# Attention and mixture-of-experts block on one core: two small operations per tile move to GpSimd, the shared weights are split earlier, the padding goes out in one DMA per expert, and the last experts are split at later places

## The reference

```python
x = x + xattn(ctx, ctx, layernorm(x))       # 16 heads of 16, 64 context rows a batch, softmax, Wo, bias
x = x + ffn(layernorm(x))
# ffn, on z = layernorm(x), n = 2048 rows:
shared = (sum over 2 shared experts of gelu(z @ sw1 + sb1) @ sw2 + sb2) / 2
gates  = z @ router_w + router_b            # 8 experts, the two highest of each row are kept
probs  = softmax(two highest)
moe    = sum over the two of probs * (gelu(z @ w1[e] + b1[e]) @ w2[e] + b2[e])
ffn    = shared + moe
layernorm(x) = (x - mean) / sqrt(var + 1e-5)
```

## Time and profile before

| what | value |
|---|---|
| median of 3 runs | 378.89 us (376.57 to 379.51) |
| the profiled execution, its own time | 380.21 us |
| its span, first to last instruction | 378.5 us |
| mean granted TensorE clock | 0.965 of full speed |
| PE busy | 326.7 us (86%) |
| DVE busy | 238.4 us (63%) |
| ACT busy | 223.0 us (59%) |
| POOL busy | 184.1 us (49%) |
| DMA | 36.93 MB, mean 98 GB/s |

### The profile page before, as it was taken

How to read it: one execution, slowest core, us unless ns; L and a number is a source line. 1 busy time by engine, 2 the same in 40 slices (tenths; PEclk the granted TensorE clock), 3 DMA queues, 4 the chain that set the end, 5 groups by cost and what they waited for, 6 DMA issues and landing times.

```text
span 378.5 us, 8163 instructions
## 1 busy us (share of the span) xinstructions
PE 326.7 (86%) x2306; PEld 275.1 (73%) x2306; DVE 238.4 (63%) x504; ACT 223.0 (59%) x407; POOL 184.1 (49%) x230
## 2 busy tenths in 40 slices
PE   4979998875888999983798999998999999999940
PEld 3757766643657878872787897997989999988830
DVE  0589999999826467870566546665666666666530
ACT  1265578756576866731566457666677677676530
POOL 4326799999632587767000001454534544535540
PEclk9998999999899999998599999999999999999995
DMA  8960000060000923346741303354453553554231
GB/s 263 404 240 3 3 0 31 28 237 0 3 2 4 351 78 135 119 144 186 275 154 55 127 0 73 57 85 75 69 86 72 73 86 70 73 86 72 29 43 14
DMA packets 23930, 36.93 MB, mean 98 GB/s; under 512 B 4400, under 2 KB 18096, under 8 KB 23504
## 3 DMA queue, kind: packets, MB, share of 16 engines
q1 hardware_dynamic: 16000, 25.06, 20.1%
q0 software_dynamic: 7456, 10.04, 15.7%
q10 hardware_dynamic: 432, 1.31, 0.9%
HBM read 23.21 MB, written 13.19 MB: 96 GB/s over the span
## 4 chain that ended last, share of the span: by engine, by line
PE 57%; DVE 10%; DMA 8%; issue 8%; POOL 6%; ACT 5%; SPq 3%; ACTq 0%; DVEq 0%; POOLq 0%
PE psS L1102 12%; PE psP L1127 11%; PE psS L1053 8%; PE psS L967 5%; PE psP L967 5%; DMA out<-xres,xg 4%; PE psS L1114 3%; POOL Pr L423 2%; PE psP L1028 2%; PE psD L902 2%; PE psS L918 2%; DVE mx L777 1%; DMA wraw<-in_w 1%; SPq L264 1%; PE psD L1003 1%
## 5 line engine op out<-in xcount | busy, mean ns | idle before, releaser
L470 POOL DMA_INDIRECT out<-xres,xg x39 | 61.0, 1563 | 58.5 <-DVE xres L869 41.2
L825 DVE TENSOR_TENSOR h_lo<-g,h_hi 128x512 fp32r<-128x512 f32 x32 | 22.1, 692 | 51.7 <-ACT h_hi L573 37.3
L1127 PE MATMUL psP<-w_lo,h_hi 128*128 x156 | 47.2, 303 | 3.3 <-DVE h_lo L877 3.3
L855 DVE TENSOR_TENSOR sraw<-psS,b1T 128x512 f32<-128x512 f32 x39 | 27.0, 692 | 33.2 <-PE psS L1114 32.2
L1127 PE MATMUL psP<-w_hi,h_hi 128*128 x156 | 43.8, 281 | 0.0
L1127 PE MATMUL psP<-w_hi,h_lo 128*128 x156 | 43.7, 280 | 0.0
L570 ACT ACTIVATE g<-psS,sb1T 128x512 f32<-128x512 f32 x32 | 22.0, 687 | 32.6 <-PE psS L1053 32.2
L423 POOL TENSOR_TENSOR Pr<-Pr,inv 128x1024 f32<-128x1024 f32 x16 | 31.3, 1954 | 19.6 <-DVE inv L814 19.6
L608 ACT ACTIVATE g<-sraw 128x512 f32<-128x512 f32 x39 | 24.6, 632 | 26.3 <-DVE sraw L855 26.2
L1102 PE MATMUL psS<-w_lo,xt_hi 128*128 x78 | 34.3, 439 | 1.2 <-issue 1.1
L600 ACT ACTIVATE sraw<-psS 128x512 f32<-128x512 f32 x39 | 23.3, 598 | 20.2 <-PE psS L1102 20.2
(11 more groups left out here) (197 smaller groups left out, 934.5 us busy)
## 6 DMA issues: line engine op xcount, KB each, us to landing
wraw<-in_w SPq DMA_DIRECT2D x16, 512.0 KB, 6.1
xg<-xg_d SPq DMA_DIRECT2D x39, 130.0 KB, 2.1
sraw<-in_sw SPq DMA_DIRECT2D x2, 1024.0 KB, 10.7
out<-xres SPq DMA_DIRECT2D x4, 512.0 KB, 3.4
xres<-in_x SPq DMA_DIRECT2D x3, 512.0 KB, 9.1
xTs<-in_xT SPq DMA_DIRECT2D x3, 512.0 KB, 9.8
xg_d<-filler SPq DMA_DIRECT2D x8, 128.0 KB
s_free<-in_b SPq DMA_DIRECT2D x1, 1024.0 KB, 4.7
```

Source lines behind the costliest of these rows:

```text
L470: pool.indirect_dma_start(out, bass.IndirectOffsetOnAxis(ap=xg[:, t % NXB, D:D + 1].bitcast(U32), axis=0), y[:, t % NYB], None, compute_op ...
L825: V.tensor_tensor(out=h_lo[:, n % 2], in0=g[:, n % 2], in1=h_hi[:, n % 2].bitcast(F32), op=ALU.subtract).then_inc(hlo_done, 1)
L855: V.tensor_tensor(out=hb[:, n % 2], in0=four(hT_bank[n % 2]), in1=b1T[:, bass.ds(e, 1), :].squeeze(1).unsqueeze(2).to_broadcast([P, HC, P] ...
L1127: last = T.matmul(res_bank[n % 2], a[:, n % 2, c * P:(c + 1) * P], b[:, bass.ds(e, 1), C * HF + c * D:C * HF + (c + 1) * D].squeeze(1), st ...
```

## The change

- `ve1`, `ve2` and `nm2` are made on POOL, right before the powers; DVE's `variance` and the two operations of each pair are gone. POOL waits for DVE's `mv1` and `mv2`.
- ACT makes `s_hi` from step 2, POOL `s_lo` from step 3.
- The filler tile has the spare row's index in its own column 256; `pad_row` and its DMA are gone. SP issues eight padding DMAs, and waits for them only before the gathers of the routed tiles. The waits of SP for the padding, for POOL's fillers and for `lean` ahead of expert 5's load are gone; ACT waits for both kinds of padding ahead of its first copy for expert 5, which overwrites `filler`.
- The pieces of experts 5, 6 and 7 go to chunks 19 and 20, 23 and 24, 27 and 28 on ACT (17 and 19, 22 and 23, 25 and 26 before); the last four on DVE to 28 and 29 (27 and 28 before).
- POOL scatters three tiles a step instead of two in steps 20 to 22.

Left out below are the lists of names that lose `pad_row`, and a count of constants that goes from 20 to 19 on PE.

```diff
--- before.py
+++ after.py
@@ -52,8 +52,8 @@
 HALF_T, HALF_G = NT // 2, NG // 2
 NYB, NX, NB = 6, 3, 3
 SPLIT_X = {5: 1, 10: 2, 18: 3}
-HIGHS = {2: 2, 3: 2, 4: 2, 6: 2, 7: 1, 8: 2, 9: 2, 11: 2, 12: 2, 13: 2, 14: 1, 17: 2, 19: 2, 22: 2, 23: 2, 25: 2, 26: 2}
-LOWS = {5: 1, 6: 2, 7: 2, 10: 1, 14: 1, 15: 2, 16: 2, 17: 1, 18: 1, 19: 2, 20: 2, 21: 2, 22: 2, 23: 2, 24: 2, 25: 1, 26: 2, 27: 2, 28: 2}
+HIGHS = {2: 2, 3: 2, 4: 2, 6: 2, 7: 1, 8: 2, 9: 2, 11: 2, 12: 2, 13: 2, 14: 1, 19: 2, 20: 2, 23: 2, 24: 2, 27: 2, 28: 2}
+LOWS = {5: 1, 6: 2, 7: 2, 10: 1, 14: 1, 15: 2, 16: 2, 17: 1, 18: 1, 19: 2, 20: 2, 21: 2, 22: 2, 23: 2, 24: 2, 25: 1, 26: 2, 28: 2, 29: 2}
 
 
 def routing_constants(lay):
...
...
@@ -259,17 +258,13 @@
             store(0)
 
             sp.wait_ge(fill_ready, 1)
-            sp.wait_ge(consts, 20)
+            sp.wait_ge(consts, 19)
             for e in range(NE):
                 r = sp.value_load(fill_i[0:1, e:e + 1], min_val=0, max_val=FILL_ROW - P)
-                sp.dma_start(xg_d[bass.ds(r, P), 0:D], filler[:, 0:D]).then_inc(fill_out, 16)
-                sp.dma_start(xg_d[bass.ds(r, P), D:ROW], pad_row[:]).then_inc(fill_out, 16)
-
-            sp.wait_ge(fill_out, 16 * 2 * NE)
+                sp.dma_start(xg_d[bass.ds(r, P), :], filler[:]).then_inc(fill_out, 16)
+
             sp.wait_ge(tabs_ready, 3)
             sp.wait_ge(slots_ready, 2)
-            sp.wait_ge(lean_done, 2)
-            sp.wait_ge(fillers, 16 * 7)
             for half in range(2):
                 expert(5, half)
             store(1)
@@ -277,18 +272,18 @@
             sp.wait_ge(xlo_done, NG)
             for half in range(2):
                 expert(6, half)
+            def tile_in(t):
+                r = sp.value_load(row_tab[0:1, t:t + 1], min_val=0, max_val=FILL_ROW + P)
+                if t >= NXB:
+                    sp.wait_ge(y_out[(t - NXB) % NW], 16 * ((t - NXB) // NW + 1))
+                sp.dma_start(xg[:, t % NXB], xg_d[bass.ds(r, P), :]).then_inc(xg_in[t % NXB], 16)
+
             for h in range(2):
                 for k in range(2):
                     sp.wait_ge(scattered[h][k], 16 * HALF_T)
             for half in range(2):
                 expert(7, half)
-
-            def tile_in(t):
-                r = sp.value_load(row_tab[0:1, t:t + 1], min_val=0, max_val=FILL_ROW + P)
-                if t >= NXB:
-                    sp.wait_ge(y_out[(t - NXB) % NW], 16 * ((t - NXB) // NW + 1))
-                sp.dma_start(xg[:, t % NXB], xg_d[bass.ds(r, P), :]).then_inc(xg_in[t % NXB], 16)
-
+            sp.wait_ge(fill_out, 16 * NE)
             sp.wait_ge(acc_stored, 16 * 2)
             for t in range(EARLY):
                 tile_in(t)
@@ -328,6 +323,9 @@
                                pattern=[[-1, P]], channel_multiplier=1).then_inc(consts, 1)
 
             def rstd1(b):
+                pool.wait_ge(mv1_done, TPB * (b + 1))
+                pool.tensor_tensor(out=ve1[:, b * TPB:(b + 1) * TPB], in0=mv1[:, b * TPB:(b + 1) * TPB, 1], in1=eps[:].to_broadcast([P, TPB]),
+                                   op=ALU.add).then_inc(ve1_done, 1)
                 pool.wait_ge(ve1_done, b + 1)
                 pool.tensor_tensor(out=rs1[:, b * TPB:(b + 1) * TPB], in0=ve1[:, b * TPB:(b + 1) * TPB],
                                    in1=half[:].to_broadcast([P, TPB]), op=ALU.pow).then_inc(rs1_done, 1)
@@ -342,7 +340,6 @@
                 pool.memset(ones[:], 1.0).then_inc(consts, 1)
                 pool.memset(filler[:], 0.0).then_inc(consts, 1)
                 pool.memset(idle[:], 0.0).then_inc(consts, 1)
-                pool.memset(pad_row[:], 0.0).then_inc(consts, 1)
                 for i in range(2):
                     pool.memset(rows[i][:, :, D:ROW], 0.0).then_inc(consts, 1)
                 pool.memset(onef[:], 1.0).then_inc(consts, 1)
@@ -355,17 +352,17 @@
                 pool.iota(unused_f[:], pattern=[[0, (TILES + 1) // 2], [P, 2]], base=FILL_ROW, channel_multiplier=0,
                           allow_small_or_imprecise_dtypes=True).then_inc(consts, 1)
                 pool.iota(ids[:], pattern=[[P, NT]], base=0, channel_multiplier=1).then_inc(consts, 1)
-                pool.wait_ge(consts, 15)
+                pool.wait_ge(consts, 14)
                 pool.affine_select(out=tri[:], in_=tri[:], compare_op=ALU.is_ge, fill=-1.0, base=-1,
                                    pattern=[[1, P]], channel_multiplier=-1).then_inc(consts, 1)
                 pool.iota(idle[:, :, 0].bitcast(I32), pattern=[[P, 2]], base=TOK + P, channel_multiplier=1).then_inc(consts, 1)
-                pool.iota(pad_row[:, 0:1].bitcast(I32), pattern=[[0, 1]], base=TOK, channel_multiplier=1).then_inc(consts, 1)
+                pool.iota(filler[:, D:D + 1].bitcast(I32), pattern=[[0, 1]], base=TOK, channel_multiplier=1).then_inc(consts, 1)
                 for i in range(2):
                     pool.tensor_copy(rows[i][:, :, D].bitcast(I32), ids[:, i * HALF_T:(i + 1) * HALF_T]).then_inc(consts, 1)
 
             def fill_unused(k):
                 if k == 0:
-                    pool.wait_ge(consts, 20)
+                    pool.wait_ge(consts, 19)
                 if k < 2:
                     unused = xg_d[FILL_ROW + k * P:FILL_ROW + (k + 1) * P, :]
                     pool.dma_start(unused[:, 0:D], filler[:, 0:D]).then_inc(fillers, 16)
@@ -402,6 +399,9 @@
                     rstd1(s // TPB)
                 if s % 2 == 0 and 5 <= s - 1 < NT + 5:
                     t = s - 6
+                    pool.wait_ge(mv2_done, t + 2)
+                    pool.tensor_tensor(out=ve2[:, t:t + 2], in0=mv2[:, t:t + 2, 1], in1=eps[:].to_broadcast([P, 2]), op=ALU.add).then_inc(ve2_done, 1)
+                    pool.tensor_tensor(out=nm2[:, t:t + 2], in0=mv2[:, t:t + 2, 0], in1=minus[:].to_broadcast([P, 2]), op=ALU.mult).then_inc(ve2_done, 1)
                     pool.wait_ge(ve2_done, t + 2)
                     pool.tensor_tensor(out=rs2[:, t:t + 2], in0=ve2[:, t:t + 2], in1=half[:].to_broadcast([P, 2]), op=ALU.pow).then_inc(pow2_done, 1)
                     pool.wait_ge(pow2_done, t // 2 + 1)
@@ -415,8 +415,8 @@
                     pool.tensor_scalar(out=sbh[:], in0=sbh[:], scalar1=1.0 / NSH, scalar2=None, op0=ALU.mult).then_inc(sbh_done, 1)
                 if 8 <= s < 13:
                     fill_unused(s - 8)
-                if 7 <= s < 7 + NSH * PPE:
-                    shared_low(s - 7)
+                if 3 <= s < 3 + NSH * PPE:
+                    shared_low(s - 3)
                 if 1 <= s <= NT:
                     t = s - 1
                     pool.wait_ge(inv_done, t + 1)
@@ -430,7 +430,7 @@
                     pool.wait_ge(slots_ready, 1)
                     pool.wait_ge(weights_done, 1)
                 if s >= NT + 4:
-                    for t in range(2 * (s - NT - 4), min(2 * (s - NT - 3), HALF_T)):
+                    for t in range(3 * (s - NT - 4), min(3 * (s - NT - 3), HALF_T)):
                         scatter(0, t)
             pool.wait_ge(scattered[0][0], 16 * HALF_T)
             weigh(0, -0.5)
@@ -516,6 +516,9 @@
             def high(i):
                 e, k = PIECES[i]
                 act.wait_ge(w_in[e][k // 2], 16)
+                if e == 5 and k == 0:
+                    act.wait_ge(fill_out, 16 * NE)
+                    act.wait_ge(fillers, 16 * 7)
                 A.activation(w_cols(w_hi[:, e], k), w_cols(wraw[e], k), ACT.Copy).then_inc(hi_done[e], 1)
 
             def tile_high(t):
@@ -554,8 +557,8 @@
                     t = s - 6
                     act.wait_ge(rs2_done, t // 2 + 1)
                     A.activation(row(t)[:, 0:D], xres[:, t], ACT.Identity, scale=rs2[:, t:t + 1], bias=nmr[:, t:t + 1]).then_inc(rows_done, 1)
-                if 6 <= s < 6 + NSH * PPE:
-                    shared_high(s - 6)
+                if 2 <= s < 2 + NSH * PPE:
+                    shared_high(s - 2)
                 if s == NT - 2:
                     x_high(0)
                 if s == NT:
@@ -635,11 +638,6 @@
                 dve.wait_ge(st1_done, t + 1)
                 V.bn_aggr(mv1[:, t], st1[:, t]).then_inc(mv1_done, 1)
 
-            def variance(b):
-                dve.wait_ge(mv1_done, TPB * (b + 1))
-                V.tensor_tensor(out=ve1[:, b * TPB:(b + 1) * TPB], in0=mv1[:, b * TPB:(b + 1) * TPB, 1], in1=eps[:].to_broadcast([P, TPB]),
-                                op=ALU.add).then_inc(ve1_done, 1)
-
             dve.wait_ge(mean_psum, 1)
             V.tensor_tensor(out=WqT[:], in0=Wq[:], in1=psA[:, 0:D].unsqueeze(1).to_broadcast([P, C, D]), op=ALU.subtract).then_inc(wq_done, 1)
             dve.wait_ge(k_psum, 1)
@@ -650,7 +648,6 @@
                 stats(t)
             for t in range(TPB):
                 aggregate(t)
-            variance(0)
 
             routed = [0]
 
@@ -781,10 +778,6 @@
                     V.bn_aggr(mv2[:, t], st2[:, t]).then_inc(mv2_done, 1)
                 if s + TPB < NT:
                     stats(s + TPB)
```

(13 more changed lines are left out.)

## The result

The changed kernel takes 365.56 us (median of 4 runs, 364.98 to 366.06) against 378.99 (376.57 to 379.51), a ratio of 0.9652 with a 95% interval of 0.9613 to 0.9692. The forecast was 365.2. The profiled execution of after took 365.25. In the table of the experiments the medians are of all executions and the ratios of the fast ones alone (a slow one is over 1.5% longer than the fastest of its kernel), so a ratio need not be the quotient of two medians there, and the profile of e5 is of a slow one.

The account below looks back on a forecast made before the run. It saw attention held by DVE and POOL together and a stall of ACT waiting 11.0 us for expert 5's weights. 11.6 + 2.5 - 0.4 = 13.7 off 380.21 gave 366.5 profiled, 365.2 as median; range 361 to 371.

Parts of the forecast that it names:

- the 2.5 of attention: Attention loop: its end at 99.8 where 102.32 stood, a gain of 2.5 us, with bounds from gain 4.5 to loss 1.2.
- SP's period of 1.4 and issue at 167.5: SP's queue: one padding DMA an expert every 1.4 us, not 1.91, so expert 5's load leaves about 167.5, 5.9 earlier.
- Chunks 17 to 21 at 4.05 and 2.82, gain 11.6: Shared chunks: without ACT's wait for expert 5, one step of 4.05 then 2.82 each; chunk 21 at 178.9, not 190.54.
- Later places at no cost: Chunks 23, 24, 27, 28: two weight copies (1.15) beside two Gelu passes (1.2) fit into 2.82, so zero cost.
- Expert 7's load: Behind the last scatter (178.69): there by 196.7 with 9.0 each for landing and load, before its copy at 198.3; zero cost.
- 0.2 for each POOL operation: Attention: each of the 20 eps and sign instructions moved to POOL takes 0.2 us; upper bound 0.72.
- Third limit: four turns of 4.81 from 80.6 to 99.8: Late attention: POOL 2.0 later by step 10, eviction at 80.6, then ACT and PE's loop sets 4.81 a turn; gain 2.5.
- the 5.5 that the prediction named as a sign of being wrong: Attention evictions after step 12: the prediction is wrong if they still step by more than 5.5 us.
- Loss 0.4 in the last pairs: Last two pairs of attention tiles: two POOL operations of 0.2 come in series before the power, a loss of 0.4.
- The reason for the 2.5: Attention: DVE's eps additions wait until POOL pauses, so removal is worth more than its work, 5.4 us in two alone.
- attention gives nothing: Rival, chance 0.14: POOL is as full as DVE and gets what DVE loses; 0 to -1.2 instead of 2.5, 367.7 to 369.
- Routed tiles at no change: Routed stage after the chunks: the change touches nothing there but its start.

Follow-up runs that it names:

- e5: Kernel before with one padding DMA an expert, the moved waits and three scatters a step, old places kept: 376.91 us, 0.9885 of before on chip 2.
- e4: Kernel before with one padding DMA an expert, moved waits, three scatters a step and later places, attention as before: 366.86 us, 0.9711 of before on chip 1.
- e9: The changed kernel, unaltered, run on the third chip: 376.2 us, 0.9787 of the kernel before there.
- e1: Kernel before with only eps and the sign of the mean moved from DVE to POOL: 379.0 us, 1.0006 of before on chip 1.
- e2: Kernel before with only the shared weights split early, from step 2 on ACT and 3 on POOL: 375.99 us, 0.9940 of before on chip 1.
- e11: Changed kernel with POOL's shared low parts at steps 3, 4, 5, 7, 9, 11, 13, 15 and its padding DMAs at 16 to 20: 373.27 us, 0.9706 of before.
- e12: One padding DMA an expert, moved waits and three scatters a step on the kernel before, old places, third chip: 378.38 us, 0.9852 of before.

## Why the prediction was right

Right in time and sign, and in the mechanism of the stall, which is 11.6 of the 13.7. The mechanism given for the 2.5 of attention was wrong in one half. That the forecast meets the median to 0.4 us is in part luck: the span fell by 15.0, of which 1.7 in the routed tiles stand in no step, attention gave 1.65 instead of 2.1, and 1.5 of the span's gain is missing between the medians. By its own steps:

- **SP's period of 1.4 and issue at 167.5.** Measured 9.11 for eight, so a period of about 1.25 ((9.11 - 0.38) / 7), and issue at 164.84, or 1.0 earlier than the 165.85 that the step gives once the front's 1.65 is taken off.
- **Chunks 17 to 21 at 4.05 and 2.82, gain 11.6.** Measured 4.03 and 2.82, 24.11 - 12.50 = 11.6; e4 gives it alone. The copy had no wait, so its room is shown only to be above zero.
- **Later places at no cost.** Two copies fit in a step of 2.82 (chunks 19, 20, 23, 24, 27, 28). Right.
- **Expert 7's load.** Expected by 196.7 at worst; it was issued at 184.73 and 185.1 and landed in time for the copy at 196.57. The scatters came out 3.1 later instead of earlier, which the step did not foresee: I had costed them at zero and had not asked what the earlier load of expert 5 would do to the ones issued behind it. It took part of a margin and no time.
- **0.2 for each POOL operation.** Measured 0.186 to 0.204 in all twelve additions. Here that is 0.20 against 0.16 free on DVE. The Trainium skill, "GPSIMD Engine Reference", section "Engine selection", has such work about 2x slower on GpSimd; for tiles this small it was not, and the measurement decides.
- **Third limit: four turns of 4.81 from 80.6 to 99.8.** The eviction came at 79.81, the end at 99.78: POOL's products were 1.25 later there instead of 2.0, and the last turn took 5.45 instead of 4.8. The gain of 2.5 at this place is right, by two errors that cancel, which is luck. On the third chip the last turn took 5.9 in e9 (93.80 to 99.71), over the 5.5 that the prediction named as a sign of being wrong; what sets this one turn was not looked for.
- **Loss 0.4 in the last pairs.** It came elsewhere: chunks 0 to 17 keep their intervals to 0.15 us, but 2.54 at step 16 became 1.65 at chunk 0. In the window 90 to 100 the granted clock is 0.91 and in the same window of before 0.83; I took no experiment on that piece, so its cause is argued at best.
- **The reason for the 2.5 was wrong in one half.** I wrote that the held additions make the removal count for more than its arithmetic. After the change no DVE instruction of the attention loop takes over 1.25 us, and DVE got 8 us of its time back (48.64 to 40.70 in 50 to 100), but the move was worth nothing: 1.0006, and 0.9773 without it against 0.9787 with it. The gain is the split's. The rival "attention gives nothing" was false of the change and true of this part of it. The Trainium skill, "Perfetto Trace Analysis", section "Optimizing Scalar/DVE Operations", warns that a move between these two may not help. e1, with its 1.0006, agrees.
- **Routed tiles at no change.** They were 1.7 faster, which no step has. In the other kernels with this code unchanged the time from ACT's first routed operation to the end goes from 152.6 to 155.1, and is the same to 0.2 us for one kernel on two chips (153.3 and 153.1 for after). No run was made to find what sets it: open.

## What to carry to other kernels

Where two engines are both full, the one whose instructions are stretched need not be the one to relieve (DVE here, e1): take away from the engine that goes from one instruction to the next without a pause, in the steps where it does so (e2, e11), and try each move alone. A transfer in an in-order queue leaves when what stands in front of it has left (the load of expert 5, 8.6 us earlier); when it leaves earlier, look at what else is in flight then. Measure on more than one chip before a ratio is quoted: here it was 0.965 and 0.979.

## What was not expected of the hardware

**One stretch differs between chips.** After takes 365.6 us in the first measurement and 376.2 on chip 3, and nearly all of the difference lies in chunks 10 to 17, where POOL issues the scatters and SP the padding. (On which of the chips the first measurement ran is not known; its intervals from chunk 10 to 17 are those of e4 on chip 1.) All kernels on chips 2 and 3 take 6.2 to 11.2 us longer there. Each has waits of ACT's Gelus put to "remote", but their sum doesn't follow the delay: 10.6 us in e5 for a delay of 7.5, 2.1 in e12 for one of 10.6. Each chip was used in one session, so chip and time are not told apart. A window of e9 and its granted clock:

```profile
165.00:170.00 5.00, 2.55 (x12) 2.55 (x13) 3.23 (x10) 2.94 (x5) 4.10 (x4) 0.54 0.48 160
```

The clock is 0.54 there, behind 4.3 us in which PE had nothing to do (up to 167.45), the second such pause within 15 us. The kernel before loses 5.3 us on that chip (384.3 against 379.0) and after 10.6; it would fit that half of the delay falls into the stall of before, where ACT waits anyway, but this is argued and not shown. So the change is worth 0.965 in the first measurement and 0.979 on the third chip. What the engines wait for isn't shown; no trace of before on those chips exists.

**Scatters beside a weight load.** POOL's wait for the landing of its scatters went from 1.7 to 4.9 us once 1 MB of weights and a store were issued before it ended. The other runs go the same way. In e4, where the load leaves at 166.33 and the wait ends at 172.64, it is 5.6. In all others the load leaves only after the wait has ended, by 2.0 to 8.2 us, and it is 1.6 to 2.8. No run moved the load alone, and what holds the scatters was not tried.
